# First targets read from SBUF, a ready-made shift comparison, and a third of the one-hots on GpSimd

## The reference

```
m   = silu(einsum(h[dst], attr, W_msg));         agg[src] += m        # message
msg = einsum(attr, W_conv, h[src]);              agg[dst] += msg      # convolution
e   = e + ln(mlp([e, n[src], n[dst]]));          agg[dst] += e        # two MLP rounds, 64 wide
out = segment_sum(xw[src] * norm, dst)                                # GCN, two layers
```

## Time and profile before

| | |
|---|---|
| runs | 21119.7, 21149.3, 21134.87 us; median 21134.87 |
| the profiled execution's own time | 21156.59 us |
| its span, first to last instruction | 21154.8 us |
| granted TensorE clock, mean of the span | 0.803 |
| busy share: PE, PEld, DVE, ACT, POOL | 76%, 68%, 67%, 38%, 25% |
| instructions | 583167 |

### The profile page before, as it was taken

One profiled execution on the slowest core, in us unless ns is written; L12 is line 12 of the kernel. 1 busy time (PEld: TensorE's weight loads), 2 busy tenths in 40 slices (PEclk: granted clock), 3 DMA queues, 4 the chain that ended last, 5 costly groups with the idle time before them and its releaser, 6 DMA issues. The chain is left out here.

```text
span 21154.8 us, 583167 instructions
## 1 busy us (share of the span) xinstructions
PE 15982.4 (76%) x211866; PEld 14338.6 (68%) x212634; DVE 14217.3 (67%) x34736; ACT 8065.5 (38%) x17256; POOL 5224.0 (25%) x3992
## 2 busy tenths in 40 slices
PE   2666666666668986999999999959999999555454
PEld 1666666666648975888888888847777777455454
DVE  3777777777749984555555555547777777677777
ACT  1444444444423333555555555523333333211111
POOL 1888888888821100000000000000000000011010
PEclk9655555555559987999999999979999999766666
DMA  2222222222215532333333333325555555255454
GB/s 57 51 53 54 51 55 51 54 52 51 55 39 145 147 113 78 109 105 110 108 108 106 110 107 108 106 70 159 157 159 158 160 157 158 66 155 153 133 152 136
DMA packets 1482423, 2200.03 MB, mean 104 GB/s; under 512 B 773750, under 2 KB 960900, under 8 KB 1438480
## 3 DMA queue, kind: packets, MB, share of 16 engines
q1 hardware_dynamic: 1168296, 1839.20, 28.0%
q0 software_dynamic: 139040, 67.50, 3.7%
q10 hardware_dynamic: 173744, 272.32, 3.6%
HBM read 1651.47 MB, written 523.16 MB: 103 GB/s over the span
## 5 line engine op out<-in xcount | busy, mean ns | idle before, releaser
L753 POOL DMA_INDIRECT records<-e_sort_rec,e_sort_index x3300 | 4362.6, 1322 | 1064.7 <-issue 1051.6
L2298 PE MATMUL e_s_ps_g<-e_s_parts,e_s_pick 128*128 128x64 bf16 x65340 | 2868.2, 198 | 680.8 <-DVE e_s_to_hot L1933 325.6
L2298 PEld LDWEIGHTS e_s_ps_g<-e_s_parts,e_s_pick 128*128 128x128 bf16 x65340 | 2628.0, 102 | 837.6 <-issue 497.2
L2409 POOL DMA_INDIRECT e_s_spill<-send,e_s_lists x220 | 212.2, 964 | 10063.6 <-DVE e_s_g_sb L1953 5465.3
L2303 PE MATMUL e_s_ps_g<-e_s_window,e_s_to_hot 128*128 128x64 bf16 x23100 | 1958.0, 198 | 4.5 <-issue 4.5
L1085 PE MATMUL e_sort_acc<-e_sort_thirds,e_sort_hot 128*128 128x48 f32 x7260 | 1574.7, 414 | 366.5 <-DVE e_sort_hot L915 366.5
L1949 DVE COPY e_s_g_sb<-e_s_ps_g 128x512 f32<-128x512 f32 x880 | 606.7, 689 | 1841.7 <-PE e_s_ps_h L2321 1333.2
L1085 PEld LDWEIGHTS e_sort_acc<-e_sort_thirds,e_sort_hot 128*128 128x128 f32 x7260 | 1557.0, 332 | 398.9 <-DVE e_sort_hot L915 398.9
L2303 PEld LDWEIGHTS e_s_ps_g<-e_s_window,e_s_to_hot 128*128 128x128 bf16 x23100 | 1251.1, 101 | 6.4 <-issue 6.2
L1932 DVE TENSOR_SCALAR e_s_pick<-e_s_rows,lane_below 128x1024 bf16<-128x1024 bf16 (+1 forms) x3300 | 1244.8, 435 | 0.0
L1230 DVE TENSOR_SCALAR e_s_pick<-e_s_rows,lane_below 128x4224 bf16<-128x4224 bf16 x660 | 868.2, 1316 | 529.2 <-DMA e_s_first<-in_dst 529.0
(11 more groups left out here) (548 smaller groups left out, 36469.7 us busy)
## 6 DMA issues: line engine op xcount, KB each, us to landing
e_s_rows<-rows_d SPq DMA_DIRECT2D x330, 1088.0 KB, 5.2
e_s_hot<-hots_d SPq DMA_DIRECT2D x550, 560.0 KB
e_s_states<-states SPq DMA_DIRECT2D x880, 256.0 KB, 3.9
e_s_to_rows<-rows_d SPq DMA_DIRECT2D x220, 608.0 KB, 6.0
e_s_rows<-rows_d SPq DMA_DIRECT2D x220, 544.0 KB, 4.7
e_s_rows<-rows_d SPq DMA_DIRECT2D x220, 512.0 KB, 5.5
e_s_to_rows<-rows_d SPq DMA_DIRECT2D x220, 512.0 KB, 6.4
states<-e_s_first_t ACTq DMA_DIRECT2D x440, 256.0 KB, 2.1
```

The source lines that it names most:

```text
L753: pool.indirect_dma_start(records, bass.IndirectOffsetOnAxis(ap=index[x][:, t:t + 1], axis=0), rec[x][:, t, :], None,).then_inc(written[x] ...
L2298: pe.matmul(to_, pick[p][:, h, here], parts[:, SPAN * c + h, r, :], start=h == 0 and r == 0, stop=False)
```

## The change

- The 110 first targets stay in SBUF (`block_firsts`) for the whole program, and SP's register loads read them there.
- The setup writes the differences of neighbouring first targets (`block_back`) to DRAM (`back_d`). Each pass loads one difference a lane (`back`) where it loaded the first target (`first`), and one `is_equal` against a constant ramp (`ramp128[p, c] = c - p`) makes the shift matrix. Two DVE instructions of each block fall away in all sorted passes, and a wait between them.
- In `sorted_gcn` and `sorted_conv` POOL makes the third pick, behind its indirect DMA; PE's `gather` and SP's load of the next `rows` into the same buffer wait for it by a semaphore of its own (`q`).

```
 setup
+            sp.wait_ge(ordered, 4)
+                sp.dma_start(back_d.rearrange("r o -> o r"), block_back[:, :]).then_inc(backs_out, 16)
+            sp.wait_ge(backs_out, 16)
+            pool.tensor_scalar(ramp128[:, :], iota128[:, :], lane[:, 0:1], None, ALU.subtract).then_inc(consts, 1)
+            dve.memset(block_back[:, 0:1], 0.0)
...
+    def first_target(sp, k):
+        return sp.value_load(block_firsts[0:1, k], min_val=0, max_val=N - 1)
 every sorted pass, SP (two places in each)
-                at = sp.value_load(dst_block[w, 0:1], min_val=0, max_val=N - 1)
+                at = first_target(sp, w)
-                sp.dma_start(first[x][:, :], dst_block[w, 0:1].broadcast_to([LANES, 1])).then_inc(loaded_[x], 16)
+                sp.dma_start(back[x][:, :], back_d[w, 0:1].broadcast_to([LANES, 1])).then_inc(loaded_[x], 16)
 every sorted pass, DVE (message: in sum_, the others: in shifts)
-                if before:
-                    dve.wait_ge(sh.sem, sh.end(k - 1))
-                dve.tensor_tensor(first_ids[:, :], iota128[:, :], first[x][:, :].broadcast_to([LANES, LANES]), ALU.add).then_inc(sh.sem, 1)
-                dve.tensor_tensor(columns[x][:, :], lane[:, 0:1], first[x][:, :], ALU.add).then_inc(sh.sem, 1)
-                dve.wait_ge(sh.sem, sh.at("columns", k))
-                dve.tensor_scalar(shift[x][:, :], first_ids[:, :], columns[1 - x if before else x][:, :], None, ALU.is_equal).then_inc(sh.sem, 1)
+                dve.tensor_scalar(shift[x][:, :], ramp128[:, :], back[x][:, :], None, ALU.is_equal).then_inc(sh.sem, 1)
 sorted_gcn and sorted_conv, SP's load
                     sp.wait_ge(v.sem, v.end(k - 2))
+                    sp.wait_ge(q.sem, q.end(k - 2))
 sorted_gcn and sorted_conv, DVE's body
-                    pick_(k, x, 2)
 sorted_gcn and sorted_conv, PE's gather
                 pe.wait_ge(v.sem, v.at("pick_own", k))
+                pe.wait_ge(q.sem, q.end(k))
 sorted_gcn and sorted_conv, POOL's body, behind the indirect DMA
+                if before >= 2:
+                    pool.wait_ge(t.sem, t.end(k - 2))
+                    pool.sem_inc(pool_tick, 1)
+                pool.tensor_scalar(pick[x][:, SPAN - 1, :], rows_[x][:, 0:OWN * LANES], lane_below[:, SPAN - 1:SPAN], None, ALU.is_equal).then_inc(q.sem, 1)
```

More of the change, by code:

```diff
@@ L339, in _ @@
             load(dec_b1[:, :], ins["L2_gnn_dec_b1"].unsqueeze(0).broadcast_to([P, F]))
+            sp.wait_ge(ordered, 4)
+            with nc.allow_non_contiguous_dma(reason="how far each block's first target lies behind the one before"):
+                sp.dma_start(back_d.rearrange("r o -> o r"), block_back[:, :]).then_inc(backs_out, 16)
+            sp.wait_ge(backs_out, 16)
         @block.scalar
@@ L583, in sorted_message @@
             cs = Chain(sem(f"{name}_message_s"), 0, ["row", "gap", "source", "weight", "attrs", "silu"])
-            bv = Chain(sem(f"{name}_sum_v"), 0, ["upper", "top", "diagonal", "above", "lower", "first", "columns", "shift", "last", "high",
+            bv = Chain(sem(f"{name}_sum_v"), 0, ["upper", "top", "diagonal", "above", "lower", "shift", "last", "high",
                                                  "middle", "low"]
@@ L900, in sum_ @@
                                              op0=ALU.mult, op1=ALU.add).then_inc(bv.sem, 1)
[L901 to L904, removed]
+                    dve.tensor_scalar(shift[x][:, :], ramp128[:, :], back[x][:, :], None, ALU.is_equal).then_inc(bv.sem, 1)
                     message_ = s[:, :, 11:11 + F]
@@ L1128, in sorted_gcn @@
         table_in, sums_out, flushed = shared(f"gcn_table_in"), shared(f"gcn_sums_out"), shared(f"gcn_flushed")
-        v = chain(shared(f"gcn_pick_v"), [f"pick{h}" for h in range(SPAN)] + ["pick_own"])
-        sh = chain(shared("gcn_shift_v"), ["first", "columns", "shift"])
+        v = chain(shared(f"gcn_pick_v"), [f"pick{h}" for h in range(SPAN - 1)] + ["pick_own"])
+        q = chain(shared(f"gcn_pick_p"), ["pick_last"])
+        sh = chain(shared("gcn_shift_v"), ["shift"])
         s = chain(shared(f"gcn_values_v"), [f"summed{g}" for g in range(len(GROUPS))] + ["values_own", "values", "values_spill", "rest0", "rest1"])
@@ L1146, in sorted_gcn @@
         lists_ = tiles("lists", [LANES, LIST_SRC + 1])
-        first = tiles("first", [LANES, 1], I32)
+        back = tiles("back", [LANES, 1])
         window, window_in = tiles("window", [LANES, F]), tiles("window_in", [LANES, F])
@@ L1395, in sorted_conv @@
         table_in, sums_out, flushed = sem(f"{name}_table_in"), sem(f"{name}_sums_out"), sem(f"{name}_flushed")
-        v = Chain(sem(f"{name}_pick_v"), 0, [f"pick{h}" for h in range(SPAN)] + ["pick_own"])
-        sh = Chain(sem(f"{name}_shift_v"), 0, ["first", "columns", "shift"])
+        v = Chain(sem(f"{name}_pick_v"), 0, [f"pick{h}" for h in range(SPAN - 1)] + ["pick_own"])
+        q = Chain(sem(f"{name}_pick_p"), 0, ["pick_last"])
+        sh = Chain(sem(f"{name}_shift_v"), 0, ["shift"])
         s = Chain(sem(f"{name}_product_v"), 0, [f"summed{g}" for g in range(len(GROUPS))] + ["own_out"] + [f"product{g}" for g in range(len(GROUPS))] + ["product_spill", "weight0", "less0", "weight1", "weight2"])
@@ L1569, in body @@
                         dve.wait_ge(t.sem, t.end(k - 2))
-                    for h in range(SPAN):
+                    for h in range(SPAN - 1):
                         pick_(k, x, h)
@@ L1724, in sorted_mlp @@
         vx = chain(shared("mlp_window_v"), ["part0", "less0", "part1", "part2"])
-        vs = chain(shared("mlp_shift_v"), ["first", "columns", "shift"])
+        vs = chain(shared("mlp_shift_v"), ["shift"])
         vm = chain(shared("mlp_merge_v"), ["scaled", "count", "rest", "both", "merged_out"])
@@ L1754, in sorted_mlp @@
         ready = tile("ready", [LANES, 1])
-        first, columns, shift = tiles("first", [LANES, 1], I32), tiles("columns", [LANES, 1]), tile("shift", [LANES, LANES])
-        first_ids = tile("first_ids", [LANES, LANES])
+        back, shift = tiles("back", [LANES, 1]), tile("shift", [LANES, LANES])
         stat = tile("stat", [LANES, 3, 2 * CELLS])
@@ L2003, in shifts @@
                 if before:
[L2004 removed]
                     dve.wait_ge(ts.sem, ts.end(k - 1))
[L2006 to L2009 removed]
+                dve.tensor_scalar(shift[:, :], ramp128[:, :], back[x][:, :], None, ALU.is_equal).then_inc(vs.sem, 1)
             def merge(k, x, before):
```

58 lines of the change are left out of this document (25 added, 33 removed).

## The result

The changed kernel takes 23,454.8 us (median of 4 runs, 23,447.4 to 23,458.0), the kernel before 21,131.9 us beside it (4 runs, 21,119.7 to 21,149.3). The ratio is 1.1098, with an interval of 1.1079 to 1.1117: 11% slower. The profiled execution has a span of 23,453.7 us, 2,299 us more than before.

The account below looks back on a forecast made before the run. It took SP's register loads to hold up GCN (11.30 us a turn), and full POOL, DVE or PE elsewhere. GCN -242, convolution -72, MLP -25, setup +3 gave -336, so 20,800 us; range 20,250 to 21,700.

Parts of the forecast that it names:

- The first rival: GCN and convolution: POOL's picks are long and DVE stands still; 21,780 us at 7 us a pick; chance 0.32.
- the length X of POOL's pick: Third pick on POOL, GCN and convolution: 4.4 us taken for 4,224 elements, unmeasured, from neighbouring POOL instructions.
- the point where the sign turns: GCN and convolution: the summed change crosses zero when POOL's pick takes 5.05 us, if DVE's two-operand instructions wait too.
- case (a): GCN: only picks on DVE and POOL exclude each other, other DVE work goes on; 9.5 us a turn.
- case (b): GCN: DVE's instructions with two SBUF operands also wait for POOL's pick; 10.75 us a turn.
- the formula: With DVE's two-operand work waiting: GCN turn 6.35 + X, convolution turn 10.8 + X - 3.0 us, X being POOL's pick.
- The cover of 3.0 us: Convolution: DVE work up to the products, needing no shared port, that would run beside POOL's pick; 3.0 us.
- Register loads: SP's two loads a block cost 0.9 instead of 5.8 us; DVE's 2.56 us wait in GCN goes, nothing elsewhere.
- SP's new wait for POOL's pick: SP's loads wait for POOL's pick of two blocks ago; costed at nothing, as it ends over a turn early.
- Shift: Two DVE instructions fewer, 0.39 us a block; nothing in the message pass, 25 us gained in the MLP rounds.
- The floor: Convolution: PE's busy time keeps the turn near 12.2 us, against 12.85 before.
- The third pick's 1.22 us: GCN and convolution: DVE is freed of 1.22 us a turn; its GCN work would be 7.13 us.

Follow-up runs that it names:

- the probe: Changed kernel with the third pick back on DVE, plus setup tests of single POOL instructions and POOL's pick beside single DVE instructions; 20,511.1 us with them in it.
- the first experiment: Changed kernel with the third pick made by DVE again in GCN and convolution and the new semaphore gone; 20,430.0 us, ratio 0.9671.

## Why the prediction was wrong

It said 20,800 us and faster; it is 23,455 and slower, beyond the range's end of 21,700. The first rival came true, in its far part and a little beyond it.

**The step that failed** is the length X of POOL's pick: "I take 4.4 us, between the near rows." It is 10.98 us. The near rows were a cast (0.83 ns an element) and a compare-and-select with a pattern instead of a scalar (1.09 ns), and neither is this instruction. The probe's copy agrees with the cast, and its `tensor_scalar` is three times as dear in every type. The far end, 10.1 us from the small compare-and-select with its start, was nearest; I had kept it as an end only, and the measured length lies beyond even that. The text had put the point where the sign turns at 5.05 us, 15% above the value it took, with nothing measured between: a chance of 0.32 for the rival was too small for that, and the range left out just the half of it that came.

The Trainium skill (GPSIMD Engine Reference, "Performance versus the Vector engine") gives 1.03 cycles an element for short single-input bodies and about 2.6 for two inputs; at its 1.2 GHz the second is an estimate of 2.2 ns. The single-input instruction here measured 2.54 ns, near the second and beyond it, and its 10.98 us lie beyond the 3.8 to 7.3 us that the prediction estimated from the Trainium skill (the 2.03 cycles for compare and select stand in the same GPSIMD Engine Reference under "Performance pitfalls for Q7 kernels").

The length outweighs the choice of case. By the prediction's own walk through the turns case (a) gives 16.1 us a turn at 10.98 us, case (b) 17.3, where the forecast had 10.2 and the row has 17.40: of the 7.2 us between them the length makes up 6.6.

**Exclusion: case (b) holds, and more strictly than it was written.** DVE's picks and two-operand instructions wait until POOL's pick ends. I had left `pick_own` and the shift out, as work that runs beside it; they wait too (10.88 and 10.96 us). The rule of the Trainium skill quoted in the prediction (SBUF — State Buffer, "Who interferes with whom") agrees with all five rows of the probe: compare, pick and two-operand instructions block for the whole instruction, the reduction doesn't. Whoever weighs a rule like this should let it choose the case: here it stood in a sentence beside the sum, which took a middle of (a) and (b).

**What the formula gives at the measured length.** GCN: 6.35 + 10.98 = 17.33 us a turn; the row is 17.40. The convolution: 10.8 + 10.98 - 3.0 = 18.8; measured (8,704.7 - 6,359.4) / 109 = 21.5. The cover of 3.0 us doesn't exist, since the shift stands in it and waits: 10.8 + 10.98 = 21.8. That GCN comes out within 0.1 us is luck. The formula takes the mean of two gaps, one with no cover and one with 2.4 us. In the changed kernel POOL gets the gap behind `rest1` in nearly every turn. The merge covers some of its pick, but the reductions stand behind `pick_own`, which waits: the cover is 8.26 - 1.22 + 10.98 - 17.40 = 0.62 us. The sum would have been 220 x 6.03 + 110 x 5.93 - 22 = +1,957 us, against +2,299 in the spans. (At X = 10.1 the same formula gives +1,667, not the "some +2,000" in the rival's text. At X = 5 it gives 21,120 us, not 21,080 as the forecast's upper end, and the middle of 9.5 and 10.75 is 10.1, not 10.2; neither changes the outcome.)

**Register loads: right.** DVE's wait on SP is gone, and what comes next is DVE's own work. From 8.74 us of work less 0.39 for the shift I had 8.35 without the pick's edit; the first experiment has 8.26. A load takes 0.27 us, less than the 0.45 taken for it. Alone they are worth 551 us of GCN, and no gain in the other stages, as said. SP's new wait for POOL's pick, costed at nothing, costs nothing that shows: DVE's picks in GCN wait 2.9 us for loads in all 220 blocks. Whether it would count in a shorter turn no run tells.

**Shift: right in GCN, too small in the convolution, too large in the MLP.** In GCN it counts once the loads are fast: GCN takes 1,911 us in the first experiment and 2,005 with the loads alone, 0.43 us a block. In the convolution I had credited nothing to it by itself, and it gives 81 us. The floor that I set there, 12.2 us from PE's busy time, was too high: the first experiment's turn is (7,671.2 - 6,358.2) / 109 = 12.05 us, with PE 99.5% and DVE 99.1% busy from 6,600 to 7,600 us. For the MLP I took -25 us. The first and the last indirect DMA of the two MLP rounds lie 9,865 us apart before, 9,871 in the changed kernel, 9,876 with the shift alone and 9,891 in the first experiment: no gain shows. Why it is up to 26 us more in single profiles stays open.

**The third pick's 1.22 us** left DVE as said, and 10.5 to 11 us of standing still came in for it.

## What to carry to other kernels

An operation may go to GpSimd beside a busy VectorE only if VectorE's work around it is of a kind that was seen to run beside it, here reductions; otherwise nearly its whole length is added to the path. And that length must be measured for that very instruction, since a neighbour's rate can be a third of it. When a sum changes sign close to the value you took for an unmeasured term, the honest forecast is the spread of that term. And where a bundle of edits loses, price them one by one: here one edit hid a gain of 3.3%, and ScalarE could take part of the work without a collision.

## What the runs showed that was not expected

- POOL's `tensor_scalar` costs 2.54 ns an element, the same for bf16 and f32, `is_equal` and `mult`, a constant and a per-lane scalar, while its copy takes 1.94 us for 2,112 elements (0.92 ns each with the start).
- A DVE instruction of 16 elements a lane took 8.87 us beside POOL's pick. The profile counts this as busy time of DVE, so no wait is listed: the sign is the mean duration of a group that has grown from 0.28 to 10.7 us.
- A register load by SP from a DRAM input was 2.5 to 3.3 us with its pointer; from SBUF it is 0.27 us.
